# A four-layer graph network on one core: layer 0 in the other order, heads 4 to 7 stacked by direct transfers, values in the attention's fill

## What is computed

```python
deg = jnp.sum(adj, axis=-1, keepdims=True)
agg = jnp.einsum('bij,bjf->bif', adj, x) / jnp.maximum(deg, EPS)
out = jax.nn.relu(jnp.einsum('bnf,of->bno', jnp.concatenate([x, agg], axis=2), W))
```

```python
scores = jnp.einsum('bhqd,bhkd->bhqk', q, k) * SCALE * (adj + adj)[:, None]
ctx = jnp.einsum('bhqk,bhkd->bhqd', jax.nn.softmax(scores, axis=-1), v)
```

## Time and profile before

| | |
|---|---|
| median of 3 runs | 3451.12 us |
| profiled execution | 3450.14 us, span 3448.3 us |
| TensorE busy | 3168.9 us (92%) |
| VectorE busy | 2149.7 us (62%) |
| ScalarE busy | 1749.3 us (51%) |
| mean granted clock of TensorE | 0.957 of full speed |
| DMA | 252.43 MB, 73 GB/s over the span |

### The profile page before, as it was taken

How to read it: one execution, slowest core, us unless ns; L and a number is a source line. 1 busy time by engine, 2 the same in 40 slices (tenths; PEclk the granted TensorE clock), 3 DMA queues, 4 the chain that set the end, 5 groups by cost and what they waited for, 6 DMA issues and landing times.

```text
span 3448.3 us, 79514 instructions
## 1 busy us (share of the span) xinstructions
PE 3168.9 (92%) x27032; PEld 2727.9 (79%) x27032; DVE 2149.7 (62%) x3916; ACT 1749.3 (51%) x3025; POOL 405.7 (12%) x1613
## 2 busy tenths in 40 slices
PE   6999989999899998999989999899997999989998
PEld 5887779877798677986779877798776987779877
DVE  4636866268662685637856378553786537865387
ACT  3425844258442684426844268432674326743277
POOL 0101110011100111000110001100111001110011
PEclk9999999999999999999999999899998999989999
DMA  5113132131320313303133031330313303123120
GB/s 198 50 54 85 48 124 64 41 84 48 124 79 29 84 45 124 97 14 88 42 121 99 13 87 47 116 99 13 87 48 114 99 25 78 57 103 98 36 49 17
DMA packets 147694, 252.43 MB, mean 73 GB/s; under 512 B 11047, under 2 KB 112172, under 8 KB 147244
## 3 DMA queue, kind: packets, MB, share of 16 engines
q1 hardware_dynamic: 147244, 246.73, 22.2%
HBM read 146.03 MB, written 100.66 MB: 72 GB/s over the span
## 4 chain that ended last, share of the span: by engine, by line
PE 45%; issue 40%; DMA 5%; DVE 4%; POOL 3%; ACT 2%; DVEq 1%; SPq 0%; POOLq 0%; ACTq 0%
PE ps L655 10%; PE ps L645 7%; PE ps L454 7%; PE ps L456 7%; PE ps L455 7%; PE ps L668 5%; DMA qk_spill<-u_lo 3%; DMA k_stack<-qk_spill 2%; PE ps L683 1%; POOL shift L427 1%; POOL vare L420 1%; DVE r L1307 1%; DVE stats L1104 1%; DVE xr L1338 1%; POOL rstd L423 0%
## 5 line engine op out<-in xcount | busy, mean ns | idle before, releaser
L1307 DVE CUSTOM_DVE_ANT_0 r<-ps,adjn 128x1024 f32<-128x1024 f32 x512 | 621.9, 1217 | 31.5 <-PE ps L655 19.5
L1014 ACT ACTIVATE r<-r,nmax 128x1024 f32<-128x1024 f32 x512 | 585.7, 1144 | 80.7 <-POOL nmax L446 80.7
L655 PEld LDWEIGHTS ps<-ident,r 128*128 128x128 f32 x4096 | 471.0, 142 | 118.6 <-DVE pt L1316 75.6
L655 PE MATMUL ps<-ident,r 128*128 128x128 f32 x4096 | 551.3, 278 | 3.5 <-DVE pt L1316 3.5
L454 PE MATMUL ps<-u_hi,t_hi 128*128 128x256 f32 x1536 | 447.0, 291 | 4.1 <-DVE u_lo L1067 4.1
L455 PE MATMUL ps<-u_lo,t_hi 128*128 128x256 f32 x1536 | 439.0, 286 | 0.0
L456 PE MATMUL ps<-u_hi,t_lo 128*128 128x256 f32 x1536 | 438.8, 286 | 0.0
L1316 DVE COPY pt<-ps 128x512 f32<-128x512 f32 x512 | 353.1, 690 | 136.3 <-PE ps L655 136.2
L645 PE MATMUL ps<-k_stack,q_stack 96*128 96x512 f32 x1024 | 377.9, 452 | 54.5 <-DVE mmax L1307 32.4
L816 ACT ACTIVATE pt<-ps 128x512 f32<-128x512 f32 x512 | 304.9, 595 | 180.1 <-PE ps L655 175.4
L454 PE MATMUL ps<-w_hi,xt_hi 128*128 128x256 f32 x1024 | 302.0, 295 | 32.3 <-DVE xt_lo L1074 27.1
(11 more groups left out here) (172 smaller groups left out, 5556.1 us busy)
## 6 DMA issues: line engine op xcount, KB each, us to landing
adjn<-in_adj SPq DMA_DIRECT2D x64, 512.0 KB, 3.4
t_spill<-t_hi SPq DMA_DIRECT2D x64, 512.0 KB, 2.6
t_spill<-t_lo SPq DMA_DIRECT2D x64, 512.0 KB, 3.7
t_hi<-t_spill SPq DMA_DIRECT2D x32, 1024.0 KB, 5.4
t_lo<-t_spill SPq DMA_DIRECT2D x32, 1024.0 KB, 8.0
q_stack<-qk_spill SPq DMA_DIRECT2D x24, 512.0 KB, 6.9
k_stack<-qk_spill SPq DMA_DIRECT2D x24, 512.0 KB, 7.6
xn<-in_x SPq DMA_DIRECT2D x16, 512.0 KB, 4.0
```

Of the source, the lines that this page charges most:

```text
L655: last = pe.transpose(ps[:, TP + half, t * P:(t + 1) * P], r[:, u % RSLOTS, (TPH * half + t) * P:(TPH * half + t + 1) * P], ident)
L1014: act.activation(r[:, s % RSLOTS, :], r[:, s % RSLOTS, :], ACT.Exp, bias=nmax[:, s % 4:s % 4 + 1], accum_out=prow[:, qt % 2, h:h + 1]).the ...
L1307: dve.tensor_tensor_reduce(out=r[:, s % RSLOTS, :], in0=ps[:, 2 * (s % 2):2 * (s % 2) + 2, :].rearrange("p a c -> p (a c)"), in1=adjn[:, q ...
```

## The change

Layer 0 is computed as adj (x W) / degree instead of (adj x) W / degree. TensorE transposes adj tiles and x in a new order, now into four banks (4, 5, 2, 3 in turn); x W ("g", eight tiles in four pairs) is projected in between and becomes u_hi and u_lo. Then `row_product` runs over the eight row tiles, with the self part x W of tile t+2 behind row tile t; the first two self parts stand ahead. ScalarE copies the self part out, VectorE multiplies the row tile by 1/degree and adds it. The eight degree sums stand in one block behind the last residual of the fill. The split of xn and the eviction of the aggregate are gone. ScalarE takes the banks of the fill in the same order as VectorE (its hunk is cut below).

For heads 4 to 7, 24 DMAs of 32 partitions x 4 KB go from u_hi and u_lo straight to the stacks, in order of heads, with a semaphore for each head; scores(4) to scores(7) wait for their own head, the first copies to pt for all of them, and SyncE waits for all before it loads xr. The DRAM tensor between is gone. The value projections, one pair a step, and their copies stand in steps 0 to 3 of the pipeline. Before the loop TensorE waits for the last copies of the constants. Counts of semaphores follow; hunks with them alone are left out.

```diff
@@ -48,13 +48,16 @@
-    TP_L0 = sum([halves_of("adj", j) for j in range(NT)], []) + x_units(0, 0) + x_units(0, 1)
+    adj_units = lambda *js: sum([halves_of("adj", j) for j in js], [])
+    TP_L0 = adj_units(0, 1) + x_units(0, 0) + adj_units(2, 3) + x_units(0, 1) + adj_units(4, 5, 6, 7)
...
+        if n < len(TP_L0):
+            return ((4, 5, 2, 3)[n % 4],)
@@ -65,7 +68,7 @@
-    PR_ORDER = ([("layer 0", t) for t in range(NT)] +
+    PR_ORDER = ([("g", k) for k in range(PAIRS)] + [("layer 0", t) for t in range(NT)] +
@@ -344,17 +341,18 @@
-                for n in range(2):
-                    sp.wait_ge(pr_free, nth(b, PR_UNITS, pr["qk", (1, n, 1)] + 1))
-                    at = slice(n * N, (n + 1) * N)
-                    sp.dma_start(qk_d[n, 0], f32(u_hi[:, at])).then_inc(qk_out[n], 16)
-                    sp.dma_start(qk_d[n, 1], f32(u_lo[:, at])).then_inc(qk_out[n], 16)
-                    sp.wait_ge(qk_out[n], nth(b, 32, 32))
-                    hi, lo = (qk_d[n, k].rearrange("(g p) n -> p g n", p=HD) for k in range(2))
-                    stack = q_stack if n == 0 else k_stack
-                    for part, src in enumerate((hi, hi, lo) if n == 0 else (lo, hi, hi)):
-                        sp.dma_start(f32(stack[HD * part:HD * (part + 1), G:2 * G, :]),
-                                     src).then_inc(stacked[n], 16)
+                for g in range(G):
+                    rows = slice(HD * g, HD * (g + 1))
+                    for n in range(2):
+                        if g == 0:
+                            sp.wait_ge(pr_free, nth(b, PR_UNITS, pr["qk", (1, n, 1)] + 1))
+                        at = slice(n * N, (n + 1) * N)
+                        hi, lo = f32(u_hi[rows, at]), f32(u_lo[rows, at])
+                        stack = q_stack if n == 0 else k_stack
+                        for part, src in enumerate((hi, hi, lo) if n == 0 else (lo, hi, hi)):
+                            sp.dma_start(f32(stack[HD * part:HD * (part + 1), G + g, :]), src).then_inc(stacked[g], 16)
+                for g in range(G):
+                    sp.wait_ge(stacked[g], nth(b, 16 * 6, 16 * 6))
@@ -550,6 +543,8 @@
+                elif n >= 2 and PR_ORDER[n - 2][0] == "layer 0":
+                    pe.wait_ge(pr_act, nth(b, NT + PAIRS, PR_ORDER[n - 2][1] + 1))
@@ -605,12 +592,14 @@
+                name, k = {AF_L0: ("g", 0), AF_P2: ("z", NT), AF_C3: ("conv 2", 2 * NT)}[af]
...
+                    if t == 0 and af == AF_L0:
+                        pe.wait_ge(tp_free, nth(b, TP_UNITS, tp_a(0, j) + 2))
@@ -636,9 +625,8 @@
-                if u == G:
-                    pe.wait_ge(stacked[0], nth(b, 16 * 3, 16 * 3))
-                    pe.wait_ge(stacked[1], nth(b, 16 * 3, 16 * 3))
+                if G <= u < 2 * G:
+                    pe.wait_ge(stacked[u - G], nth(b, 16 * 6, 16 * 6))
@@ -660,6 +648,8 @@
+                if grp == 0 and part == 0:
+                    pe.wait_ge(pr_free, nth(b, PR_UNITS, PR_UNITS))
@@ -690,28 +680,31 @@
+            pe.wait_ge(set_act, 12)
...
-                for j in range(NT):
-                    if j + 1 < NT:
-                        transpose_adj(b, 0, j + 1)
-                    pe.wait_ge(tp_free, nth(b, TP_UNITS, tp_a(0, j) + 2))
-                    if j % TPH == 0:
-                        pe.wait_ge(x_split, nth(b, 2, j // TPH + 1))
-                    transposed_products(j)
-                transpose_x(b, 0)
+                transpose_adj(b, 0, 1)
+                transpose_x_half(b, 0, 0)
+                transpose_adj(b, 0, 2)
+                transpose_adj(b, 0, 3)
...
+                project_pairs(b, "g", W_L0G, xt_wait(b, 0), range(2))
+                transpose_x_half(b, 0, 1)
+                transpose_adj(b, 0, 4)
+                transpose_adj(b, 0, 5)
+                project_pairs(b, "g", W_L0G, xt_wait(b, 0), range(2, PAIRS))
+                transpose_adj(b, 0, 6)
+                transpose_adj(b, 0, 7)
+                self_part = lambda t: project(pr_bank(b, pr["layer 0", t])[:, 0:F], W_L0X, t).then_inc(pr_full, 1)
+                self_part(0)
+                self_part(1)
...
-                    if t == 0:
-                        pe.wait_ge(tp_free, nth(b, TP_UNITS, tp_x(0, 1) + 2))
-                    if t == NT - 1:
+                    row_product(b, t, AF_L0)
+                    if t + 2 < NT:
+                        self_part(t + 2)
+                    if t == NT - 3:
...
-                    dst = pr_bank(b, pr["layer 0", t])
-                    project(dst[:, 0:F], W_L0X, t)
-                    if t % TPH == 0:
-                        pe.wait_ge(u_ready, nth(b, 4 + PAIRS, 2 * (t // TPH) + 2))
-                    project(dst[:, F:2 * F], W_L0G, t, gh, gl).then_inc(pr_full, 1)
@@ -790,14 +783,15 @@
-                project_pairs(b, "values", W_V, xt_wait(b, 3))
-                pe.wait_ge(pr_free, nth(b, PR_UNITS, PR_UNITS))
+                pe.wait_ge(pr_free, nth(b, PR_UNITS, pr["qk", QK[-1]] + 1))
...
+                    if s < PAIRS:
+                        project_pairs(b, "values", W_V, xt_wait(b, 3), range(s, s + 1))
@@ -888,30 +882,27 @@
-                             xn[:, TPH * j:TPH * (j + 1), :].rearrange("p t f -> p (t f)")).then_inc(x_split_hi, 1)
...
-                    copy(gh[:, ft, half * 512:(half + 1) * 512], ps[:, ACC + k, :]).then_inc(u_act, 1)
...
+                rows_from_pr(b, "g", range(2))
...
+                rows_from_pr(b, "g", range(2, PAIRS))
...
-                        act.wait_ge(pr_free, nth(b, PR_UNITS, n - 1))
-                    copy(ev[:, t % 2, 0:F], ps[:, PR + n % 2, F:2 * F], rdeg[:, t:t + 1]).then_inc(pr_act, 1)
+                        act.wait_ge(acc_free, nth(b, 3 * NT, t - 1))
+                    copy(ev[:, t % 2, 0:F], ps[:, PR + n % 2, 0:F]).then_inc(pr_act, 1)
...
-                        x_transposed(b, 1, 0)
+                x_transposed(b, 1, 0)
@@ -994,13 +985,14 @@
-                for k in range(2):
-                    act.wait_ge(qk_out[k], nth(b, 32, 32))
...
+                        if u == 0:
+                            for g in range(G):
+                                act.wait_ge(stacked[g], nth(b, 16 * 6, 16 * 6))
@@ -1136,43 +1128,37 @@
+                adj_transposed(b, 0, 0)
+                adj_transposed(b, 0, 1)
+                x_transposed(b, 0, 0)
+                adj_transposed(b, 0, 2)
+                adj_transposed(b, 0, 3)
+                dve.wait_ge(xr_free, b + 1)
+                rows_from_pr(b, "g", U_G, range(2))
+                x_transposed(b, 0, 1)
+                adj_transposed(b, 0, 4)
+                adj_transposed(b, 0, 5)
+                rows_from_pr(b, "g", U_G, range(2, PAIRS))
+                adj_transposed(b, 0, 6)
+                adj_transposed(b, 0, 7)
...
-                        dve.wait_ge(xr_free, b + 1)
...
-                        dve.wait_ge(x_split_hi, nth(b, 2, j + 1))
-                        rest(u_lo[:, at], xn[:, TPH * j:TPH * (j + 1), :].rearrange("p t f -> p (t f)"), u_hi[:, at],
...
-                    rest(gl[:, ft, at], ps[:, ACC + k, :], gh[:, ft, at], u_ready)
...
-                        dve.tensor_tensor(ev[:, t % 2, F:2 * F], ps[:, PR + n % 2, 0:F], ev[:, t % 2, 0:F],
-                                          ALU.add).then_inc(pr_free, 1)
...
-                        raw_stats(b, 0, t - 1)
...
-                        mean_variance(b, 0, t - 1)
...
+                dve.wait_ge(deg_ready, nth(b, 2, 1))
+                for t in range(NT):
+                    dve.wait_ge(pr_act, nth(b, NT + NT // 2, t + 1))
+                    dve.sem_inc(pr_free, 1)
+                    dve.wait_ge(acc_full, nth(b, AF_PER, AF_L0 + t + 1))
+                    dve.scalar_tensor_tensor(out=ev[:, t % 2, F:2 * F], in0=ps[:, ACC + t % 4, 0:F],
+                                             scalar=rdeg[:, t:t + 1], in1=ev[:, t % 2, 0:F], op0=ALU.mult,
+                                             op1=ALU.add).then_inc(acc_free, 1)
+                    dve.wait_ge(acc_free, nth(b, 3 * NT, t + 1))
+                    relu_residual(b, 0, t)
+                    tile_stats(b, 0, t)
+                    if t == NT - 3:
@@ -1284,17 +1270,9 @@
-                dve.wait_ge(spilled, nth(b, 16 * NT, 16 * NT))
-                for k in range(NT // 2):
-                    n = pr["values", k]
-                    dve.wait_ge(pr_full, nth(b, PR_UNITS, n + 1))
-                    dve.tensor_copy(xn[:, 2 * k:2 * k + 2, :].rearrange("p t f -> p (t f)"),
-                                    ps[:, PR + n % 2, :]).then_inc(pr_free, 1)
...
-                for k in range(2):
-                    dve.wait_ge(qk_out[k], nth(b, 32, 32))
@@ -1308,8 +1286,18 @@
+                    if s < PAIRS:
+                        n = pr["values", s]
+                        if s == 0:
+                            dve.wait_ge(spilled, nth(b, 16 * NT, 16 * NT))
+                        dve.wait_ge(pr_full, nth(b, PR_UNITS, n + 1))
```

(24 more changed lines are left out.)

61 lines of the change are left out of this document (15 added, 46 removed).

## The result

The changed kernel takes 3346.73 us (median of 4 runs, 3345.47 to 3347.55) against 3451.13 for the kernel before on the same chip: a ratio of 0.9697 [0.968, 0.9714]. That is 104 us less, 11 us more than forecast; the range held it. Its profiled execution took 3346.72 us, with a span of 3345.0.

What follows compares the result with a forecast made beforehand. TensorE (92% busy) was taken as the bound, its idle and low-clock time as winnable. 8 x (5.9 layer 0 + 5.9 entry) - 1.1 = 93 us less: 3357 us profiled, 3358 median; own range 3324 to 3412, stated range 3327 to 3412.

Steps and rivals of the forecast that it cites:

- 47 and 47: Forecast savings of layer 0 and of the attention's entry, each 5.9 us an element over eight elements.
- Fill, 20.2 us from the start to VectorE's last residual: Layer 0's start: transposes into four banks, 6.6 us at low clock, VectorE's residuals from 886.4 to about 906.6.
- New wait of 1.8 us before the fifth self part: Layer 0: TensorE reaches self_part(4) at 915.8 and gets its bank at 917.6, ScalarE's copy being held by the degree sums.
- 0.9 us of low clock behind that wait: Layer 0: allowance booked for TensorE's clock dropping after the new wait, since similar pauses had gone either way.
- The bounds of 9.5 and 2.0 us: Layer 0's saving per element: 9.5 without wait or low clock, fill at VectorE's floor; 2.0 with longer fill and low clock.
- Degree block, 9.8 us: Layer 0: eight degree reductions in one VectorE block behind the fill, plus 0.7 us for two small steps.
- Entry, 5.3 + 0.6 us: Attention's entry, per element: stack copies begin 5.3 us sooner, mask 4 another 0.6 us sooner behind the first scores.
- The chain of masks and value copies: Attention's first steps: masks 0 to 3 and value copies followed in turn, mask 4 beginning 9.7 us behind the first scores.
- Transfers, 0.66 us each at 200 GB/s, six to spare: Heads 4 to 7: 24 direct transfers take 15.7 us, ending six microseconds before pt's first write, so cost nothing.
- rivals 2 and 3: Transfers at half the stack loads' rate, 3434 us (chance 0.07); or 1.7 us each, fixed part unhidden, 3506 us (0.05).
- The Trainium skill's figure: Transfers: 138 GB/s at 64 KB, by which 3.15 MB would take 23 us, ending within a microsecond of the need.
- Once, 1.1 us: Before the loop: TensorE waits for the constants' copies, ending at about 39.2 where it began at 38.0; costs 1.1 us.

Runs made afterwards that it cites:

- deg_in_fill: The changed kernel with one degree sum behind each adjacency tile of the fill instead of a block after it: 3361.54 us, 0.9737 of the kernel before.
- transfers_twice: The changed kernel with a second copy of each of the 24 transfers, to an unread DRAM tensor, also waited for: 3427.41 us.
- l0_only: The kernel before with the change's new layer 0 alone, the attention's entry left old: 3383.01 us, 0.981 of the kernel before.
- deg_split: The changed kernel with four degree sums ahead of row tile 0 and one behind each of tiles 0 to 3: 3327.81 us, run again 3326.78.
- after_again: The changed kernel, unaltered, run once more beside two variants on one chip: 3346.77 us, 0.9697 of the kernel before.
- banks2: The changed kernel with layer 0's fill in two banks (4 and 5) instead of four: 3410.87 us, 0.9898 of the kernel before.

## Why the prediction was right

- **Order of the costs.** TensorE's waits and low clock in layer 0 and in the entry were where the time went, and both are gone or smaller. Each part alone is faster in its own stretch by about its share (53 and 43 us for 47 and 47); the 68 and 52 us of the two kernels hold low clock elsewhere besides.
- **Fill, 20.2 us from the start to VectorE's last residual.** Measured 19.3 (865.45 to 884.76), with the self parts done 18.5 us behind the start (882.52 + 2 x 0.72), where 19.3 stood. Right in the main, and for the reason given: VectorE's 24 residuals nearly fill it, and deg_in_fill shows what more work on VectorE does. The low clock was booked at 6.6 us; it was 2.9 in four elements and 5.9 in three. The step was mis-sized, and it mattered little, since 3 us of it cost 0.7.
- **New wait of 1.8 us before the fifth self part.** Measured 1.28, at that place, by that chain, in all eight elements.
- **0.9 us of low clock behind that wait.** None came in any element: the clock behind the wait is 1.00 to the end of the layer. This is the largest miss in layer 0. The rows of before left it open, behind 1.74 us the one way and behind 1.48 the other; the wait here is shorter than either. 0.8 (fill) + 0.5 (wait) + 0.9 (clock) - 0.4 (row products 28.5 for 28.1) are the 1.8 us by which the third element beat its 5.9 (56.02 - 48.25 = 7.8). The mean of the elements beat it by 1.2: some have the longer low clock, and the third was the longest before. The bounds of 9.5 and 2.0 us held the measured 7.1, but they don't come out of the terms named with them: without the wait and the low clock the sum is 8.6, and the fill's share of the rest isn't worked out.
- **Degree block, 9.8 us.** Measured 9.5 (884.68 to 894.2). Its price was given as the wait alone; moving half of it gave 1.9 us an element, 0.5 of which no step accounts for.
- **Entry, 5.3 + 0.6 us.** In the third element 5.26 + 0.46; in the mean 5.3 + 0.15. The chain of masks and value copies gave mask 4 at 9.7 us behind the first scores, and it came at 9.83. It took the high clock level for granted, where the earlier trace rows had 0.67; that held (1.00).
- **Transfers, 0.66 us each at 200 GB/s, six to spare.** 193 to 217 GB/s, 7.8 to spare. The issue was mis-sized (0.61 us for 0.42, read from loads of another shape). That brought it to the 0.66 of the transfer, so that either may have set the pace, and it cost nothing. A transfer could have taken 0.33 us more (7.8 / 24) before anything waited for it; beyond that transfers_twice shows the price of rivals 2 and 3, full pay, without their cause. The Trainium skill's figure weighed above ("DMA: Bandwidth & Descriptors", section "Measured (HBM→SBUF, 128 partitions, SWDGE, issued from GpSimd)", 138 GB/s at 64 KB) would by that estimate have left a microsecond. Its table is of another route and issuer, so the 193 to 217 GB/s here don't refute it; they show that its figure doesn't carry over to 128 KB transfers queued by SyncE.
- **Once, 1.1 us.** 1.9 at the start (39.9 for 38.0), 0.6 won back at the end.
- **What the prediction had no term for.** 1.1 us less an element in layers 1 and 2 (low clock) and 0.65 more in the attention (two pauses), both in unchanged code. The 10 us that the profiled execution lies below the forecast are 10 of layer 0 and 9 of layers 1 and 2, less 4 of the entry and 5 of the pauses. So the number is as near as it is partly by luck, since these two unforeseen terms nearly cancel. The prediction also summed layer 0 and the entry as independent; alone they give 15 us more than together, most of it in unchanged code.

What stays open: the cause of the 0.35 us pauses; what decides whether an element has 10.2 us of low clock in layers 1 and 2 or 3.4 more, and whether the change had a part in its being less in the mean; why the key stack came sooner in l0_only; 0.5 us of layer 0 in deg_split and as much in deg_in_fill. No run changed these by themselves.

## What to carry to other kernels

Where an engine is starved at the start of a stage, count the buffers between it and its readers first: the new order won only with four banks. When two edits touch one wait, price them together: the moved values were worth nothing while the key stack came through DRAM, and half of the entry's gain is of the pair. Work that an engine must do once before a pipeline (the degree sums) belongs in the pipeline's own slack, as much of it as isn't needed for the first tile. Before a gain is put down to an edit, compare the stretches that it leaves alone, and their low clock: here they gave 9 us and took 5.

## What the runs showed of the hardware

- Twenty-four transfers of 128 KB from 32 partitions to 32 partitions, queued back to back, ran at 193 to 217 GB/s, about as the loads from DRAM into 32 partitions did (197). Reading from 32 partitions on top of writing to them did not halve the rate.
- The issue of such a transfer took SyncE about 0.6 us with others in flight (0.51 to 0.66 in transfers_twice). In the kernel before three loads of 512 KB took 0.42 each, and the stores of 512 KB from u_hi and u_lo 0.32 to 0.75. What sets it isn't shown.
- In the fill of layer 0, with the same instructions and no wait of TensorE before, the clock rose to 2.4 GHz after 2.9 us in some elements and after 5.9 in others, and not in the same ones in after_again. Those 3 us cost 0.7 us, since VectorE is nearly the bound there. Where TensorE had gaps of 1.18 and 0.56 us (third element of banks2) the clock was still at 0.50 after 8 us.
- The time of layers 1 and 2 goes in steps with their low clock. In the 96 elements of the twelve profiled executions, 10.2 us at the low level go with 194.3 to 194.6 us (41 elements), 13.6 with 195.5 to 196.0 (41), 17.0 with 197.1 to 197.6 (13), and 6.8 with 193.2 (1). So 3.4 us at the low level cost 1.4 us there, and an element differs from its neighbour in the same execution.
- Some pauses of about 0.35 us belong to a build of the kernel, not to its work: unchanged code of 132.6 us took 132.89 in both executions of deg_split and 133.24 in the change, in all elements alike.
